# Later groups' loads at the end of the projection's block, a group's loads behind denominators and shift, and values copied in one operation

## The reference, cut to what matters

```python
x = L0_attn_x                                   # 4 x 1024 x 128, float32
x = x + layernorm(attention(layernorm(x)))      # 16 heads of 8, relative position bias
x = x + layernorm(ffn(layernorm(x)))            # router, 64 experts, 8 per token, shared expert

# attention(x):
xn = layernorm(x) * ln_g + ln_b
q, k, v = split(xn @ w_qkv + b_qkv)             # 16 heads of 8
scores = q @ k.T * scale + rel_bias[head, i - j + t - 1]
out = softmax(scores) @ v
return out @ w_out + b_out
```

## Time and profile before

| | |
|---|---|
| time, median of 3 runs | 1193.54 us (1192.19 to 1193.61) |
| the profiled execution's own time | 1190.53 us |
| its span in the profile | 1188.6 us |
| granted TensorE clock over the span | 0.868 of full |
| busy: TensorE / VectorE / ScalarE / POOL | 74% / 66% / 58% / 50% |
| transfers on SP's queue | 87,062 packets, 68.21 MB |

### The profile page before, as it was taken

How to read it: one execution, slowest core, us unless ns; L and a number is a source line. 1 busy time by engine, 2 the same in 40 slices (tenths; PEclk the granted TensorE clock), 3 DMA queues, 4 the chain that set the end, 5 groups by cost and what they waited for, 6 DMA issues and landing times. The chain is left out here.

```text
span 1188.6 us, 16268 instructions
## 1 busy us (share of the span) xinstructions
PE 883.5 (74%) x5090; PEld 274.5 (23%) x5090; DVE 789.2 (66%) x1222; ACT 689.8 (58%) x1433; POOL 592.6 (50%) x734
## 2 busy tenths in 40 slices
PE   4653999999889999989999998999973530555400
PEld 2410222222222222222222222222211320444300
DVE  7864888889869989968988987998711320111107
ACT  4721767787767777768778776777771210322204
POOL 5820010114255555635745644555575756478747
PEclk9865999999989999999999999999996675655655
DMA  3859523012211122220001120000000010767546
GB/s 99 242 157 133 113 65 103 20 37 65 71 54 27 30 56 73 67 46 7 8 14 36 39 69 15 5 5 16 6 5 22 19 46 3 182 130 135 99 96 208
DMA packets 110379, 77.97 MB, mean 66 GB/s; under 512 B 35359, under 2 KB 95259, under 8 KB 110294
## 3 DMA queue, kind: packets, MB, share of 16 engines
q1 hardware_dynamic: 87062, 68.21, 21.9%
q0 software_dynamic: 21504, 6.79, 4.8%
q10 hardware_dynamic: 1728, 1.94, 1.0%
HBM read 38.75 MB, written 54.95 MB: 79 GB/s over the span
## 5 line engine op out<-in xcount | busy, mean ns | idle before, releaser
L209 DVE TENSOR_REDUCE half_max<-s_pair 128x2 f32<-128x1024 f32 x512 | 601.9, 1217 | 113.1 <-PE s_pair L198 109.5
L1248 ACT ACTIVATE probs<-st_bank 128x512 f32<-128x512 f32 x1024 | 543.8, 603 | 171.6 <-PE st_bank L1308 171.2
L1111 POOL DMA_INDIRECT table<-rows,keys_i x256 | 256.7, 1003 | 179.4 <-issue 68.3
L1308 PE MATMUL st_bank<-q_stack,k_stack 98*128 98x512 bf16 (+1 forms) x1024 | 326.1, 390 | 10.1 <-ACT probs L1248 7.6
L1317 PE MATMUL pv_bank<-probs,values 128*9 128x512 f32 x2048 | 270.4, 600 | 3.1 <-ACT unit_out L1182 3.0
L198 PE MATMUL s_pair<-k_stack,q_stack 64*128 64x512 bf16 x1024 | 204.0, 398 | 41.4 <-DVE half_max L209 22.0
L198 PEld LDWEIGHTS s_pair<-k_stack,q_stack 64*128 64x128 bf16 x1024 | 49.4, 93 | 359.6 <-issue 185.2
L1491 POOL DMA_INDIRECT sums<-out,ids x64 | 99.7, 1558 | 40.7 <-ACT out L1546 18.4
L1308 PEld LDWEIGHTS st_bank<-q_stack,k_stack 98*128 98x128 bf16 (+1 forms) x1024 | 78.2, 97 | 170.1 <-issue 75.8
L1505 DVE CAST ids<-xe 128x4 uint32<-128x4 f32 x16 | 2.9, 180 | 136.2 <-DMA sums<-out,ids 84.5
L1005 POOL CAST shift<-minus_max 128x16 bf16<-128x16 f32 x32 | 6.4, 201 | 111.7 <-DVE minus_max L215 111.6
(11 more groups left out here) (181 smaller groups left out, 788.4 us busy)
## 6 DMA issues: line engine op xcount, KB each, us to landing
table<-blank SPq DMA_DIRECT2D x8, 772.0 KB, 7.4
xe<-table SPq DMA_DIRECT2D x16, 386.0 KB, 4.8
q_stack<-q_image SPq DMA_DIRECT2D x96, 64.0 KB
k_stack<-k_image SPq DMA_DIRECT2D x96, 64.0 KB
s<-sums SPq DMA_DIRECT2D x24, 256.0 KB, 6.0
k_image<-k_piece SPq DMA_DIRECT2D x16, 256.0 KB, 3.3
table<-rows,keys_i POOLq DMA_INDIRECT x256
sums<-zeros SPq DMA_DIRECT2D x16, 256.0 KB
```

What stands on the lines that cost most here:

```text
L209: nc.vector.tensor_reduce(halves[:, h:HG:SIDE_HEADS, tile, half], stacks.s_pair[slot % S_SLOTS][:].rearrange("p (s k) -> p s k", s=SIDES), ...
L1111: pool.indirect_dma_start(out=table, out_offset=bass.IndirectOffsetOnAxis(ap=keys_i[c % 2][:, pick:pick + 1], axis=0), in_=rows[c % 2][:, ...
L1248: A.activation(probs[:, s % P_SLOTS, :], st_bank[at % ST_BANKS][:], ACT.Exp).then_inc(bank_free, 1)
L1308: M(bank(at)[:], k_stack[g][own, tile // PER, h, tile % PER * P:(tile % PER + 1) * P], q_stack[g][own, half, h, :], start=True, stop=True) ...
```

## The change

1. `load_values` of group 0 moves from behind chunk 6 to behind chunk 3, the waits for the stores of chunks 0 and 1 with it.
2. The loads of groups 1 and 2 for batch 0 are issued by SP at the end of block 1, behind the stores of chunk 7. In block 2 SP puts the shift of unit 0 first and then loads group 3.
3. The position rows of groups 1, 2 and 3 (30 transfers) are issued by ScalarE at the end of block 1; before, groups 1 and 2 were issued by ScalarE at the start of block 2, group 3 by SP.
4. In a unit SP sends the reciprocals and the shift first, and the group's 13 loads behind them.
5. `copy_v` copies a chunk's values in one operation of 512 columns where it took four of 128. For that the tile `vst` and the store `v_columns` hold the 16 heads of a token side by side; the tile `values` stays by groups. A group's load of values then reads 8 pieces of 144 bytes in each of 128 partitions where it read one piece of 1,152 bytes, and the store of a chunk writes one piece of 2,304 bytes in each partition where it wrote four of 576.

```diff
--- before.py
+++ after.py
@@ -123,7 +123,7 @@
         self.q_stored, self.k_stored, self.v_stored = ([sem(f"{t}_stored{a}") for a in range(2)] for t in "qkv")
 
         self.q_piece, self.k_piece = ([sb(f"{t}_piece{a}", [P, 3, CHUNK], BF16) for a in range(2)] for t in "qk")
-        self.vst = [sb(f"vst{a}", [P, GROUPS, PER, HG * VW]) for a in range(2)]
+        self.vst = [sb(f"vst{a}", [P, PER, H, VW]) for a in range(2)]
         self.half_max, self.minus_max = [sb(f"half_max{v}", [P, HG, PER, 2]) for v in range(2)], sb("minus_max", [P, HG * PER])
 
         self.s_pair = [ctx.enter_context(nc.psum_tensor(f"s_pair{v}", [P, SIDES * CHUNK], F32)) for v in range(S_SLOTS)]
@@ -144,7 +144,13 @@
 
 
 def load_values(engine, stacks, v_columns, b, g):
-    engine.dma_start(stacks.values[:, g].rearrange("p k c -> p (k c)"), v_columns[:, g, b * TILES_T:(b + 1) * TILES_T].rearrange("p k c -> p (k c)")).then_inc(stacks.loaded[g], 16)
+    engine.dma_start(stacks.values[:, g], v_columns[:, b * TILES_T:(b + 1) * TILES_T, HG * VW * g:HG * VW * (g + 1)]).then_inc(stacks.loaded[g], 16)
+
+
+def load_group(engine, stacks, q_image, k_image, v_columns, b, g):
+    for side in range(SIDES):
+        load_side(engine, stacks, q_image, k_image, b, g, side)
+    load_values(engine, stacks, v_columns, b, g)
 
 
 LOAD = 16 * (6 * SIDES + 1)
@@ -289,7 +295,7 @@
                 for first, pieces in ((0, slice(0, 2)), (2, slice(0, 3, 2))):
                     sp.dma_start(k_image[c, first:first + 2].rearrange("w d h i -> (d h) w i"), k_piece[a][:, pieces, :]).then_inc(k_stored[a], 16)
                 sp.wait_ge(v_done, c + 1)
-                sp.dma_start(v_columns[:, :, c * PER:(c + 1) * PER].rearrange("p g j d -> p g (j d)"), vst[a][:].rearrange("p g j d -> p g (j d)")).then_inc(v_stored[a], 16)
+                sp.dma_start(v_columns[:, c * PER:(c + 1) * PER, :], vst[a][:].rearrange("p j h c -> p j (h c)")).then_inc(v_stored[a], 16)
 
                 if c == 0:
                     sp.wait_ge(bias_split, 3)
@@ -302,15 +308,17 @@
                         load_bias_queries(sp, stacks, bias_q_image, 0, side)
                 elif c in (2, 3):
                     load_bias_keys(sp, stacks, bias_k_image, c - 2)
-                elif c == 4:
+                if c == 3:
                     for v in range(2):
                         sp.wait_ge(q_stored[v], 16)
                         sp.wait_ge(k_stored[v], 32)
                         sp.wait_ge(v_stored[v], 16)
-                if c in (4, 5):
+                    load_values(sp, stacks, v_columns, 0, 0)
+                elif c in (4, 5):
                     load_side(sp, stacks, q_image, k_image, 0, 0, c - 4)
-                elif c == 6:
-                    load_values(sp, stacks, v_columns, 0, 0)
+
+            for g in (1, 2):
+                load_group(sp, stacks, q_image, k_image, v_columns, 0, g)
 
         @block.vector
         def _(dve):
@@ -399,7 +407,7 @@
 
             inverse(0)
             for a in range(2):
-                G.memset(vst[a][:].rearrange("p g j (h c) -> p (g j h) c", h=HG)[:, :, HD:VW], 1.0).then_inc(ones_made, 1)
+                G.memset(vst[a][:, :, :, HD:VW], 1.0).then_inc(ones_made, 1)
             inverse(1)
             pool.wait_ge(bias_in, BIAS_CONSTS)
             G.tensor_copy(tabk_p[:, 0, :], tabk[:]).then_inc(table_split, 1)
@@ -458,9 +466,7 @@
                     act.wait_ge(v_stored[a], 16 * (c // 2))
                 if c == 0:
                     act.wait_ge(ones_made, 2)
-                for j in range(PER):
-                    ins = A.copy(vst[a][:, :, j, :].rearrange("p g (h c) -> p g h c", h=HG)[:, :, :, 0:HD], psV[a][:, j * P:(j + 1) * P].rearrange("p (g h d) -> p g h d", g=GROUPS, h=HG))
-                ins.then_inc(v_done, 1)
+                A.copy(vst[a][:, :, :, 0:HD], psV[a][:].rearrange("p (j h d) -> p j h d", j=PER, h=H)).then_inc(v_done, 1)
 
             for half in range(2):
                 act.wait_ge(bias_ready, half + 1)
@@ -478,6 +484,12 @@
                 copy_v(c)
                 if c + 2 < CHUNKS:
                     normalise(c + 2)
+            act.wait_ge(bias_stored, 16 * 6)
+            act.wait_ge(stacks.bias_rows_in[0], LOAD_BIAS[0])
+            for g in range(1, GROUPS):
+                for side in range(SIDES):
+                    load_bias_queries(act, stacks, bias_q_image, g, side)
+                    copy_bias_keys(act, stacks, g, side)
 
         @block.tensor
         def _(pe):
@@ -701,11 +713,6 @@
         MOVED, SPREAD = 16 * 2 * HG, 16 * HD
         SCATTERED = 16 * PER * TOPK
 
-        def load(sp, b, g):
-            for side in range(SIDES):
-                load_side(sp, stacks, q_image, k_image, b, g, side)
-            load_values(sp, stacks, v_columns, b, g)
-
         def put_shift(sp, n):
             _, half, g = unit_of(n)
             sp.wait_ge(bank_free, after(place["shift", n]))
@@ -741,18 +748,17 @@
                 for d in range(HD):
                     sp.dma_start(recip_t[d:P:HD, :], packed[:]).then_inc(recip_moved, 16)
 
-            load(sp, 0, 1)
             put_shift(sp, 0)
-            for g in range(2, GROUPS):
-                load(sp, 0, g)
-            for side in range(SIDES):
-                load_bias_queries(sp, stacks, bias_q_image, GROUPS - 1, side)
-                copy_bias_keys(sp, stacks, GROUPS - 1, side)
+            load_group(sp, stacks, q_image, k_image, v_columns, 0, GROUPS - 1)
             for n in range(ALL_UNITS):
                 b, half, g = unit_of(n)
                 if n >= 1:
                     move_out(n - 1)
 
+                if n >= GROUPS and g == 0:
+                    spread_reciprocals(routed(n))
+                if n < ALL_UNITS - 1:
+                    put_shift(sp, n + 1)
                 if n >= UNITS - GROUPS + 1 and (half == 1 and g >= 1 and b < B - 1 or half == 0 and g == 0 and b > 0):
                     done_b, _, done_g = unit_of(n - 1)
                     if done_b == 0 and done_g == 0:
@@ -762,11 +768,7 @@
                             sp.wait_ge(stacks.v_stored[a], 16 * CHUNKS // 2)
                     sp.wait_ge(bank_ready, after(place["step", n * STEPS - 1]))
                     sp.wait_ge(pv_done, n * TILES_T)
-                    load(sp, done_b + 1, done_g)
-                if n >= GROUPS and g == 0:
-                    spread_reciprocals(routed(n))
-                if n < ALL_UNITS - 1:
-                    put_shift(sp, n + 1)
+                    load_group(sp, stacks, q_image, k_image, v_columns, done_b + 1, done_g)
                 if n == 0:
                     for dst, src in later:
                         sp.dma_start(dst, src, allow_slow_non_contiguous=True).then_inc(later_in, 16)
@@ -1160,11 +1162,6 @@
         @block.scalar
         def _(act):
             A = nc.scalar
-            act.wait_ge(bias_rows_in[0], LOAD_BIAS[0])
-            for g in (1, 2):
-                for side in range(SIDES):
-                    load_bias_queries(act, stacks, bias_q_image, g, side)
-                    copy_bias_keys(act, stacks, g, side)
 
             def shift_copy(n):
                 at = place["shift", n]
@@ -1685,7 +1682,7 @@
     dram = lambda name, shape, dt=F32: nc.dram_tensor(name, shape, dt).ap()
     q_image, k_image = dram("q_image", [CHUNKS, 3, HD, H, CHUNK], BF16), dram("k_image", [CHUNKS, K_PLACES, HD, H, CHUNK], BF16)
     bias_q_image, bias_k_image = dram("bias_q_image", [2, 3, HD, H, CHUNK], BF16), dram("bias_k_image", [2, K_PLACES, HD, CHUNK], BF16)
-    v_columns = dram("v_columns", [P, GROUPS, TILES, HG * VW])
+    v_columns = dram("v_columns", [P, TILES, H * VW])
     table = dram("table", [SLOT_ROWS, ROW])
     sums = [dram(f"sums{v}", [ROWS, DIM]) for v in range(SUMS)]
     row = lambda a, n: a.rearrange("(o d) -> o d", o=1).to_broadcast([P, n])
```

## The result

The changed kernel takes 1157.39 us (median of 4 runs, 1155.2 to 1160.6) where the kernel before took 1192.87 beside it: a ratio of 0.9706, 95% interval 0.9679 to 0.9734, 35.5 us less. The profiled execution took 1155.2 us, its span is 1153.3: 35.3 us under the span before.

A forecast was written before the change was run, and what follows sets the result against it. TensorE bounds the middle; time is lost to its waits in the opening and units 8, 16 and 24. Gains 12.0 + 18.8 = 30.8 us from 1190.53 give 1159.7 profiled, 1162.7 as median; range 1156.5 to 1172.5.

The forecast's parts named there:

- Values earlier: Opening: with values loaded behind chunk 3, unit 0's row scores start at 69.9 instead of 73.53, 3.6 us gained.
- Loads at the block's end: Opening: issues fit beside VectorE's maxima and the first shift lands at 101.0 instead of 113.06; 12.0 us with earlier values.
- the floor of 95.6: Opening: earliest landing of the first shift if transfers don't hold it, 17.4 us before 113.06.
- the prediction's own sign: Opening: first scores for the exponential at 101 show the forecast, at 95.6 rival C.
- rival C: Opening: transfers don't hold the shift, gain 17.4 + 18.8, time 1157.3 us; chance 0.08.
- The late bound: Opening: stores and loads one after the other, shift at 104.7, gain 8.4 us; completion rule making it so given 0.15.
- Loads behind denominators and shift: Units 8, 16 and 24: reciprocals sent 7.9 us after the cut, units fall to 23.7 us, 18.8 us gained.
- What is late next: Loading units: group loads land 3.5 to some 6 us before their first reader; cost taken as nothing.
- Small pieces, one copy: Values' loads in 144-byte pieces cost 1 us for each of two loads ahead of the shift; one copy gains nothing.
- the opening's sum: Opening: 12.0 us gained, bounds 8.4 and 17.4, with 1 us for each of two small-piece loads included.

The follow-up runs named there:

- the run that used the slack up: Changed kernel with SP also waiting for the unit's last step (step 31) before issuing a group's loads; 1159.92 us, ratio 0.9727.
- the middle alone: Kernel before, with only the unit order changed: reciprocals and shift first, the 13 loads behind them; 1173.40 us, ratio 0.9856.
- the sides swapped: Kernel before, with ScalarE issuing its position rows side 1 first in each group; 1190.54 us, ratio 0.9983.
- the other group first: Kernel before, with ScalarE issuing the position rows of group 2 before those of group 1; one run, 1194.84 us.

## Why the prediction was right, step by step

**Values earlier: right.** 3.6 us expected, row scores at 69.66 against 73.53 (3.9), and the block opens 3.2 us earlier; alone it gives 2.9 to 3.7 us. The 0.7 us between lie in VectorE, see the last part.

**Loads at the block's end: the mechanism right, the size too small.** The issues lie beside the maxima as forecast (88.8 and 87.5 against 87.3 and 86.2 forecast). The step that was mis-sized is the landing of the first shift: I put it at 101.0, from a rate of 144 KB a us taken out of the old opening; it released the scores at 95.78, on the floor of 95.6 that I had kept as a bound, a gain of 17.3 where the sum has 12.0. From 80 to 88 us the transfers ran at 195 GB/s, not 144, and I had no reason but the row for holding that the old rate would stay. The old opening itself spoke against it in part: 144 KB a us was also its mean from 93 to 128 us, but in the last 8 of these the transfers' share was down to 0.76 and 0.63, and from 104 to 112 they moved 169 to 173 GB/s. By the prediction's own sign, scores at 95.6, this profile is rival C, to which I gave 0.08, and the time, 1157.39 us, is C's 1157.3 and not the forecast's. That the result lies within the stated range is owed to its wide lower end, which reached down to the floor. Over five profiles of this opening the scores start at 95.8, 97.0, 97.0, 97.3 and 99.8, a gain of 13.3 to 17.3: the transfers do hold the shift in four of them, by less than I took, so the truth lies between the forecast and C. Why the same kinds of loads are slower in the first 10 us of the old opening than in the new one stays open: swapping sides, other groups and the same group at once moved the rate by some 20 GB/s, and idle engines don't go with it either (187 and 173 GB/s in windows where they are nearly idle). How long the queues are was not tried apart.

The late bound by the Trainium skill (DMA: Bandwidth & Descriptors, "Queues, rings and completion order"), that no completion count lands before all earlier writes of its transfer engine, would have been 104.7 at the old rate. No profile reaches it. That does not speak against the rule, since the rate in the bound was wrong: at 195 GB/s the same sum, 69 + 7 + 4.13 MB / 195, gives 97.2 (an estimate from the numbers above), in the middle of the five profiles. No run here separates the queues.

Both kinds of issue had a cost of their own: with the position rows late 8 us are lost, with the loads late 4.

**Loads behind denominators and shift: right in size.** 18.8 us forecast, 18.8 in the profile, 17.8 by the move alone. The excess over the waits (12.95) went with the waits, as taken: the granted clock is 1.00 in all three units once they are gone, and 0.89 in unit 8 when the old order is put back.

**What is late next: right.** No unit waits for group data. The first reader, which I had put 28.8 us after the cut (for unit 16), comes at 28.0 in unit 15 of the run that used the slack up.

**Small pieces, one copy: nothing can be seen of the 2 us in the opening's sum.** The Trainium skill's table in the same page (DMA: Bandwidth & Descriptors, "Specifications") puts line rate at 512 bytes and more; with 144-byte pieces in place of 1,152 the time moves by less than the runs' spread (1157.39 and 1158.90 against 1156.77), so no run here shows a price. The loads of values are about a sixth of a group's 13 loads by bytes, and in the changed kernel nobody waits for them.

## What to carry to other kernels

Before a loop opens, look for what stands still while one engine finishes the stage before it: here SP, ScalarE's queue and the transfers idled through 16 us of row maxima, and some 14 of the opening's 17 us could be had from it without touching any arithmetic (the other 3 or so are the earlier values). In a queue with a fixed order put what is small and waited for ahead of what is large and needed much later, and count both the bytes and the issues ahead of it; an engine that issues transfers starts its own work only when it is through with them (ScalarE's copy at 100.04 behind 20 issues, at 90.72 without). And do not carry a transfer rate from one arrangement to another: it is the first term to give a wide range. Here it gave the largest error, 5.2 us by the first profile.

## What the runs showed that I had not expected

The transfer rate itself, at a full share of the engines, was 132 to 147 GB/s from 94 to 102 us of the old opening and 177 to 201 from 80 to 88 of the new, for the same kinds of loads; later in the old opening, from 104 to 112, it was 169 to 173.

VectorE can be slower at the end of block 1, where POOL still splits keys. The changed kernel, VectorE:

```profile
67.71 1.26 DVE L96 CAST q_piece<-q_less 128x512 bf16<-128x512 f32 x1
...
69.98 1.10 DVE L377 CAST ident<-const_ident 128x128 bf16<-128x128 f32 x1
71.00 18.18 DVE L215 TENSOR_REDUCE half_max<-s_pair 128x2 f32<-128x1024 f32 x16
```

The two casts took 0.43 and 0.16 us in the profile of the kernel before, where POOL began its last chunk only at 68.04, after the first cast and at the start of the second; here POOL works without a break from 67.2 until 71.0. The maxima start at 71.00 for it, though their first scores are there at 70.3. It isn't the change that does it: three profiles with the old block 1 (the middle alone, the sides swapped, the other group first) have the same 1.26 and 1.10 us, and the changed kernel without SP's early loads has 0.43 us for the first cast. It seems to go by when the last chunk's keys reach POOL, which varies from one profile to the next: in that of the kernel before TensorE's granted clock was 0.52 from 62 to 66 us, and the keys came later; in that of the changed kernel it was 1.00. That POOL's work is the cause is argued from the overlap, not tested.
